# Half of the float32 weight-row loads of a ternary quantiser issued from SyncE's queue instead of GpSimd's, in an attention and BitLinear kernel on eight cores

## The reference, cut to what matters

```python
def bitlinear(x, W, b):
    w_scale = clip(mean(abs(W)), 1e-5)
    Wq = clip(round(W / w_scale), -1, 1) * w_scale          # ternary weights
    x_scale = clip(max(abs(x), axis=-1), 1e-5)
    xq = clip(round(x * (127 / x_scale)), -128, 127) * (x_scale / 127)
    return xq @ Wq.T + b

x = L0_attn_x                                   # (1, 16384, 1024) float32
x = x + layernorm(attention(layernorm(x)))      # one head of 1024, softmax over 16384 keys
x = x + layernorm(bitlinear(gelu(bitlinear(layernorm(x), W1, b1)), W2, b2))
# W1: (4096, 1024), W2: (1024, 4096), float32
```

## Time and profile before

| what | us |
|---|---|
| median of the two timed runs | 5308.33 (5301.81 and 5314.85) |
| the profiled execution, slowest core | 4917.75 |
| its span (core 2, first to last instruction) | 4916.2 |
| spans of the eight cores in it | 4894.0 to 4916.2 |
| phase 1, until the first load of phase 2 | 994.5 |

### The profile page before, as it was taken

The page is one execution under the profiler, slowest core; times in us unless marked ns, Lnnn a source line. Parts: engine busy times, 40 slices in busy tenths (PEclk is TensorE's granted clock), DMA queues, the critical chain, the costliest instruction groups (busy, mean ns, idle before and its releaser), DMA issues.

```text
span 4916.2 us, 38607 instructions; the slowest of 8 cores (4894.0 to 4916.2 us)
## 1 busy us (share of the span) xinstructions
PE 2863.0 (58%) x12163; PEld 1204.5 (25%) x12406; DVE 2056.0 (42%) x2949; ACT 785.7 (16%) x1131; POOL 83.9 (2%) x162
## 2 busy tenths in 40 slices
PE   2000001569999999999999994714344544444344
PEld 1000000124444444444444441201111111111111
DVE  0677787412222222222222222625665556655665
ACT  0000000111111111111111110002222222222221
POOL 1000000000000000000000000000000000000000
PEclk8555555789999999999999997857667766677667
DMA  4998865321111111111111111330000000000000
GB/s 86 234 241 238 252 231 177 113 69 35 35 35 35 35 35 35 35 35 35 35 35 35 35 18 43 112 128 9 9 9 9 17 9 9 9 16 11 9 9 9
DMA packets 245575, 315.07 MB, mean 64 GB/s; under 512 B 164448, under 2 KB 164480, under 8 KB 241280
## 3 DMA queue, kind: packets, MB, share of 16 engines
q10 hardware_dynamic: 47232, 134.24, 9.0%
q1 hardware_dynamic: 179072, 96.50, 8.4%
q0 software_dynamic: 19072, 81.83, 5.8%
HBM read 213.95 MB, written 67.12 MB: 57 GB/s over the span
## 4 chain that ended last, share of the span: by engine, by line
PE 48%; DVE 30%; issue 8%; DMA 8%; ACT 5%; DVEq 1%; ACTq 0%; SPq 0%; POOL 0%; POOLq 0%
PE ps_s L672 18%; PE ps_z L686 9%; PE ps_z L728 9%; PE ps_h L1011 4%; PE ps_l L693 2%; DVE f1k L940 2%; DVE f1k L943 2%; DVE f1k L932 2%; DVE f1k L936 2%; DVE f1k L919 2%; DVE ln_scr L542 2%; PE ps_o L1080 2%; DVE ln_scr L539 2%; ACT f1k L923 2%; DVE hs_col L1031 1%
## 5 line engine op out<-in xcount | busy, mean ns | idle before, releaser
L672 PE MATMUL ps_s<-q_fm,k_buf 128*128 128x512 bf16 x4030 | 893.5, 380 | 31.8 <-DMA k_buf<-xn_scr 28.4
L708 DVE TENSOR_TENSOR z_acc<-ps_z,z_acc 128x512 f32<-128x512 f32 x240 | 166.0, 692 | 1149.8 <-PE ps_z L686 1148.4
L678 ACT ACTIVATE p_sb<-ps_s,c_nshift 128x512 bf16<-128x512 f32 x512 | 351.7, 687 | 1608.1 <-PE ps_s L672 1608.1
L672 PEld LDWEIGHTS ps_s<-q_fm,k_buf 128*128 128x128 bf16 x4096 | 401.5, 98 | 513.3 <-issue 32.2
L686 PE MATMUL ps_z<-v_buf,p_sb 128*128 128x512 bf16 x2006 | 452.5, 380 | 76.6 <-ACT p_sb L678 70.4
L728 PE MATMUL ps_z<-v_buf,p_sb 128*128 128x512 bf16 x1985 | 446.2, 379 | 5.5 <-PE ps_l L693 3.3
L1080 PE MATMUL ps_o<-w2q_sb,hq_fm 128*128 128x512 bf16 x992 | 352.6, 529 | 94.4 <-ACT hq_fm L1070 90.8
L1011 PE MATMUL ps_h<-w1q_sb,xq_fm 128*128 128x512 bf16 x1000 | 273.0, 419 | 67.9 <-ACT h_sb L1024 65.0
L1065 PE MATMUL ps_t<-ident,hq_bf 128*128 128x128 bf16 x512 | 52.7, 265 | 424.8 <-DVE hq_bf L1058 424.8
L420 PE MATMUL ps_k<-ones_f32col,asums 128*1 128x1 f32 x2 | 0.2, 163 | 509.3 <-DVE asums L415 509.3
L686 PEld LDWEIGHTS ps_z<-v_buf,p_sb 128*128 128x128 bf16 x2048 | 196.5, 98 | 332.7 <-issue 107.5
(11 more groups left out here) (126 smaller groups left out, 2559.8 us busy)
## 6 DMA issues: line engine op xcount, KB each, us to landing
x_tile<-x_in ACTq DMA_DIRECT2D x128, 512.0 KB, 4.8
wq_stream<-w1t POOLq DMA_DIRECT2D x16, 2048.0 KB, 11.9
xn_scr<-xn_tm ACTq DMA_DIRECT2D x128, 256.0 KB, 5.2
wq_stream<-w2t POOLq DMA_DIRECT2D x64, 512.0 KB, 4.9
v_buf<-xn_scr SPq DMA_DIRECT2D x128, 256.0 KB, 2.7
w1q_scr<-wq_out ACTq DMA_DIRECT2D x8, 1024.0 KB, 10.8
w2q_scr<-wq_out ACTq DMA_DIRECT2D x32, 256.0 KB, 3.3
xr_tile<-x_in ACTq DMA_DIRECT2D x16, 512.0 KB, 4.2
```

Of the source, the lines that this page charges most:

```text
L672: eng.matmul(ps_s[sp][:], k_buf[par][:, dc, kt * P:(kt + 1) * P], q_fm[:, dc, qg * QG:(qg + 1) * QG], start=(dc == 0), stop=(dc == DC - 1)))
L678: pl.op("scalar", lambda eng, kt=kt, sp=sp: eng.activation(out=p_sb[:, kt, :], in_=ps_s[sp][:], func=AF.Exp, scale=1.0 / 32.0, bias=c_nshi ...
L708: eng.tensor_add(out=z_acc[:, t, 0:512], in0=ps_z[qt][:], in1=z_acc[:, t, 0:512]),
```

## The change

Both loaders pick the issuing engine by the number of the block. Even blocks go to SyncE's queue, odd ones stay with GpSimd. Buffers, sizes, places in the program and the waits that the planner derives from the buffers are as before; the even ones take their place in SyncE's list, behind whatever was written there earlier.

```diff
@@ wq_load (pass a)
-            pl.op("gpsimd", lambda eng, s=src_t, i=i, par=par, cols=cols:
+            e_, q_ = ("gpsimd", "LD_G") if idx % 2 else ("sync", "LD_S")
+            pl.op(e_, lambda eng, s=src_t, i=i, par=par, cols=cols:
                   eng.dma_start(out=wq_stream[par][:, 0:cols],
                                 in_=s[i * P:(i + 1) * P, :]),
-                  writes=[bt(f"wq_stream{par}")], dma="LD_G")
+                  writes=[bt(f"wq_stream{par}")], dma=q_)
```

## The result

The changed kernel takes **1.0142 times as long** as before, with a 95% interval of 1.0125 to 1.0159: about 70 us more on 4918. The median of its nine timed runs is 4989.6 us (4980.84 to 5373.06); the profiled execution took 4977.39 us, against 4917.75 before. The sum of the prediction, made against the profiled execution, was +72.7 us, 4990 us. The number on record, 5381 us, and its whole range, 5315 to 5440, missed. Six more timed runs of the kernel before brought its median from 5308.33 down to 5186.58. In some executions of either kernel the cores of a die, or of both, have a lower granted clock (down to about 0.73 instead of 0.79) and take up to 8% longer, up to 5317 us before and 5373 after; the two timed runs that stood ahead of the prediction lie at that level, though their own clocks are not on record, and the ratio leaves such runs out.

A forecast was written before the change was run, and what follows sets the result against it. VectorE's in-order list was taken to pace phase 1. Stalls 48.4 + 21.9 + 21.6 less 19.2 given back made +72.7 us, added to the median 5308.3 for 5381 us; range 5315 to 5440.

The forecast's parts named there:

- What bounds the kernel: Phase 1: VectorE's list, run in order, sets the pace; a stall there is not made up before the barrier.
- Pass b and the later part of pass a cost nothing: Pass b, and pass a from idx 8 on: 0, with the unknown put at 10 us either way.
- Stall A: Pass a, load 0 behind sixteen transposes on SyncE's queue: VectorE waits 48.4 us for block 0, bounds 33 to 72.
- Stall B: Pass a, load 4 behind transposes g2 on SyncE's queue: VectorE waits 21.9 us, bounds 9 to 31.
- Stall C: Pass a, load 6 behind transposes g3, which follow load 4: VectorE waits 21.6 us, bounds 1 to 31.
- Given back: Between 216 and 246 us: VectorE's 19.2 us of waits for `xn_scr` stores go; the other end is none.
- The sum: Phase 1: three stalls less the waits given back, +72.7 us, ends +24 and +134; chance 0.68 for +24 to +106.
- putting the sum on the median: Whole kernel: +72.7 us added to the median shown, 5308.3, not the profiled 4917.75, gives 5381 us, 1.4% more.
- More than 2% slower: Rival, 236 to 310 us: DMA saturation stays during g2 and g3, +110 us, 5419 us; chance 0.19.
- No change: Rival, phase 1: loads held up less than thought, or time caught up; anything under +24 us; chance 0.10.
- A gain from relieving GpSimd: Rival: half the loads leave GpSimd, pass b's store waits shrink by half at best, −18 us, 5290 us; chance 0.03.

The follow-up runs named there:

- the run with pass b alone: Only pass b splits its loads between SyncE and GpSimd, pass a as in the kernel before; against that kernel, ratio 0.9996 (0.9965 to 1.0027).

## Why the prediction was right in its reasons and wrong in its number

- **What bounds the kernel: right.** VectorE's list paces phase 1; the shift of 63.6 us at block 6 was still 63.3 us at the barrier.
- **Pass b and the later part of pass a cost nothing: right**, by the run with pass b alone (0.9996), and because line 407 waits three times only, for blocks 0, 4 and 6.
- **Stall A, 48.4 us: 44.4 measured.** The sixteenth transpose was out a little earlier than worked out, since loads 0 and 2 go out at 203.39 (204.2 forecast), and load 0 landed in about 8.2 us instead of 11.5: with no tile traffic beside it a 2 MB load is faster than the row I took, which had such traffic. The transposes were 2.5 to 4.0 us apart meanwhile (3.01 forecast).
- **Stall B, 21.9 us: 17.5.** Load 4 went out at 268.46 (274 forecast) and landed in 8.6.
- **Stall C, 21.6 us: 20.1.**
- **Given back, 19.2 us: 23.6** between the two cores that the profiles show, when all waits for `xn_scr` stores are counted; up to block 6 it is 81.9 − 63.6 = 18.3. But core 2, from which I took the 19.2, had more of these waits than any other core of the kernel before (28.0 against an average of 16.0), and averaged over the cores 11.4 came back. Why they go is not shown: with two queues, spread transposes and no pause of VectorE they fall as well, to 6.0.
- **The sum, +72.7 us: +59.6 in the profiled execution, +66.0 at the start of phase 2 averaged over the cores, +70 by the ratio.** Within the sum the landing time is the mis-sized term: 3 us too long for each of the three loads, 9.4 of the 10.0 us by which the stalls came out shorter (81.9 for 91.9).
- **The step that failed: putting the sum on the median.** The base, 5308.3 us, is the mis-sized term of 5308.3 + 72.7; the ratio and the profiled execution put it at about 4918. I wrote that the profile can't say where the 390 us between the profiled execution and the median are, and added the sum to the median all the same. The gap (7.4%) was a property of those two executions and not of the kernel: its further runs go down to 4911. Three of the nine timed runs of the changed kernel, 5355.65 to 5373.06, did fall in the range, its median did not. The width of my range came from the terms in phase 1 alone, ±60 us, and had no part for this gap of 390, though I had named it. In the ratio, 1.4% forecast and 1.42% measured, it cancels. That the two agree so closely, and that 4990 is the measured median almost to the us, is partly luck: the stalls were forecast too long and the give-back too large, which offset each other in part, and the ratio itself is known only to 8 us.
- **More than 2% slower, saturation that stays: no.** The transposes of g2 were 5.3 us apart on average and those of g3 6.0, with single gaps of 10.4 and 13.9, not 12 to 14 throughout.
- **No change: no.** The Trainium skill's rule ("DMA: Bandwidth & Descriptors", section "Issuing engines are not separate DMA queues") holds for what it speaks of: where nothing stands ahead of the loads, in the run with pass b alone, two issuing engines measure the same as one (0.9996, within 0.3%). But moving a DMA to another issuer also moves its place in an order, and that was worth 1.4%.
- **A gain from relieving GpSimd: no.** Nothing of it shows in the run with pass b alone, whose interval leaves room for 17 us.

## What to carry to other kernels

Before a DMA is moved to an "idle" queue, write down that queue's list in program order and date each entry: by when it can go out, and by when its data is needed. A transfer with a deadline must not stand behind one that has none, and advancing only the first of several blocked transfers merely moves the wait to the next. Look also at what goes out earlier by the move: loads that left at 1 us delayed the tile loop by 11 to 13. Averages over all cores are safer than one core of each execution, where a difference of some 10 us is to be read. And when the profiled execution and the timed runs disagree by more than the effect in question, give the forecast as a ratio, or a range wide enough for both.

## What the runs showed of the hardware

- A small transfer on one queue can be held up by large ones on another: the 0.2 KB load of `bq_col` held GpSimd's queue for 14.6 us beside two 2 MB loads from SyncE, instead of 2.3 (12.6 to 15.4 over the eight cores), and everything serialised behind it moved with it. The kernel with spread transposes and split loads shows it again, with 15.6 on core 0.
- With VectorE standing still, seven transposes issued between 181 and 200 us took 2.7 us each to land (median), against 5.4 over the whole of the phase before; and loads of 2 MB landed in 8.3 and 8.6 us instead of 11.5. The DMA engines' share was 0.43 from 167 to 212 us, where it had been 1.08 (167 to 216). So a stalled consumer frees the DMA engines for what it waits for.
